# Layer 1 of a compressed-interaction tower regrouped by roll of h: four product tiles in full precision, twelve split in two, h's rolls passed through PSUM one after the other

## What is computed

```python
for i, (W, b) in enumerate(zip(Ws, bs)):
    z = jnp.einsum('bhd,bmd,ohm->bod', h, x, W.reshape(O, H, F))
    z = jax.nn.relu(z + b[None, :, None])
    if i < n_layers - 1:
        half = O // 2
        h, direct = (z[:, :half, :], z[:, half:, :])
    else:
        direct = z
    directs.append(direct)
out = jnp.concatenate(directs, axis=1)
return jnp.sum(out, axis=-1)
...
h = jnp.maximum(h @ W_top1 + b_top1, 0.0)
h = jnp.maximum(h @ W_top2 + b_top2, 0.0)
y = h @ W_top3
```

## Time and profile before

| quantity | value |
|---|---|
| runs of the kernel before | 1121.48, 1125.46 and 1120.56 us, median 1121.48 |
| the profiled execution | 1127.21 us |
| its span, from the first to the last instruction | 1125.4 us |
| granted TensorE clock, mean | 0.995 of full speed |
| busy, share of the span | PE 97%, DVE 92%, POOL 66%, ACT 53% |
| DMA | 162.97 MB, mean 145 GB/s |

### The profile page before, as it was taken

One profiled execution on the slowest core, in us unless ns is written; L12 is line 12 of the kernel. 1 busy time (PEld: TensorE's weight loads), 2 busy tenths in 40 slices (PEclk: granted clock), 3 DMA queues, 4 the chain that ended last, 5 costly groups with the idle time before them and its releaser, 6 DMA issues.

```text
span 1125.4 us, 11475 instructions
## 1 busy us (share of the span) xinstructions
PE 1086.0 (97%) x3562; PEld 660.5 (59%) x3562; DVE 1034.8 (92%) x580; ACT 597.8 (53%) x517; POOL 744.1 (66%) x333
## 2 busy tenths in 40 slices
PE   3789999999999999999999999999999999999997
PEld 1355655666565666656666666656665666656665
DVE  1589999999999999999999999999999999999993
ACT  0156555545654555565455556555545655555545
POOL 6466767777787777768777777877777787743110
PEclk9899999999999999999999999999999999999999
DMA  6665454665544466554446555544566554455200
GB/s 203 206 166 147 141 144 132 177 174 153 149 147 135 129 177 176 166 143 138 141 128 171 176 155 161 141 134 127 169 176 168 148 142 145 131 153 145 78 0 1
DMA packets 73576, 162.97 MB, mean 145 GB/s; under 512 B 14785, under 2 KB 39874, under 8 KB 73554
## 3 DMA queue, kind: packets, MB, share of 16 engines
q1 hardware_dynamic: 52738, 147.57, 46.2%
q10 hardware_dynamic: 12624, 10.92, 3.0%
q0 software_dynamic: 8192, 4.21, 2.3%
HBM read 95.52 MB, written 8.39 MB: 92 GB/s over the span
## 4 chain that ended last, share of the span: by engine, by line
PE 86%; DVE 6%; issue 2%; ACT 1%; DMA 1%; another core or an unknown queue 1%; ACTq 1%; POOL 1%; SPq 0%; DVEq 0%; POOLq 0%
PE z_ps L723 84%; DVE raw L591 2%; PE u_ps L723 2%; DVE prod L527 2%; DVE prod_lo L597 2%; DMA twice<-raw 1%; POOL gathered L364 1%; ACTq L1016 0%; ACT prod_hi L1097 0%; ACT h_roll L1083 0%; PE mlp_ps L723 0%; ACT h L969 0%; DMA gathered<-in_table,rows_sb 0%; DMA base_sb<-in_row_base 0%
## 5 line engine op out<-in xcount | busy, mean ns | idle before, releaser
L723 PE MATMUL z_ps<-prod,w_sb 128*128 128x512 f32 x1280 | 575.6, 596 | 10.8 <-ACT direct L959 4.0
L364 POOL DMA_INDIRECT gathered<-in_table,rows_sb x256 | 454.1, 1774 | 73.9 <-issue 68.3
L723 PEld LDWEIGHTS z_ps<-prod,w_sb 128*128 128x128 f32 x1280 | 243.6, 191 | 273.4 <-issue 262.3
L986 ACT CAST prod_hi<-raw 128x2048 fp32r<-128x2048 f32 x160 | 305.2, 1908 | 180.0 <-DVE raw L591 179.3
L591 DVE TENSOR_TENSOR raw<-h_roll,x_roll 128x2048 f32<-128x2048 f32 x160 | 363.4, 2288 | 1.2
L527 DVE TENSOR_TENSOR prod<-mlp_ps,x_roll 128x2048 f32<-128x2048 f32 x124 | 279.6, 2285 | 8.5 <-issue 5.7
L723 PE MATMUL z_ps<-prod_hi,w_hi 128*128 128x512 f32 x648 | 249.0, 464 | 3.5 <-DVE prod_lo L597 3.1
L375 POOL TENSOR_TENSOR prod_lo<-raw,prod_hi 128x2048 fp32r<-128x2048 f32 x32 | 146.8, 4587 | 135.4 <-DVE prod_lo L597 109.1
L597 DVE TENSOR_TENSOR prod_lo<-raw,prod_hi 128x2048 fp32r<-128x2048 f32 x98 | 223.9, 2286 | 1.0
L384 POOL TENSOR_TENSOR prod_lo<-raw,prod_hi 128x2048 fp32r<-128x2048 f32 x30 | 139.0, 4632 | 122.3 <-DVE prod_lo L597 122.3
L723 PE MATMUL z_ps<-prod_lo,w_hi 128*128 128x512 f32 x648 | 204.8, 396 | 0.0
...
## 6 DMA issues: line engine op xcount, KB each, us to landing
x_roll<-x_dram SPq DMA_DIRECT2D x128, 512.0 KB
...
twice<-raw ACTq DMA_DIRECT2D x128, 64.0 KB
...
```

The costliest lines, as they stand in the source:

```text
L364: nc.gpsimd.indirect_dma_start(gathered[:, u, g * DIM:(g + 1) * DIM], None, table, bass.IndirectOffsetOnAxis(ap=rows_sb[:, col:col + 1], a ...
L723: return nc.tensor.matmul(*args, **kw)
L986: nc.scalar.copy(prod_hi[:, SPLIT_SLOT[r], :, :], raw[:, RAW_SLOT[r], :, :]).then_inc(hi_ready, 1)
```

## The change

Layer 1's 16 tiles are grouped by roll of h. The four tiles of roll 0 are whole (two whole pairs, `products1`, which read h from SBUF), and the twelve tiles of rolls 1, 2 and 3 are split: six pairs A10, A12, A20, A22, A30, A32, where the first digit is the roll and the second the first of two x. ACT copies roll 1, 2 and 3 to `mlp_ps` in turn (`copy_roll`), each when the pairs of the roll before it are made, and x's base of chunk c+2 behind them. `raw` and `prod_hi` have four slots, `prod_lo` three, and `h_roll` has one copy rather than two. POOL now makes the rest of three pairs (A10, A20, A32) and DVE of three (A12, A22, A30). The half tile of layer 0 is made for chunk c+2 in step c. SP issues the rolls of h ahead of the loads of `x_roll`, and frees them by A30 and A32. The loads of the dense network's first weights move to the end. The core of the diff:

```diff
-WHOLE1 = 3
-B0, B1, A1, B2, B3 = range(5)
-SPLIT1 = 5
+WHOLE1 = 2
+A10, A12, A20, A22, A30, A32 = range(6)
+SPLIT1 = 6
 RING = 2
...
+RAW_SLOT = (0, 1, 2, 3, 0, 1)
+RAW_RING = 4
+HI_SLOT = (0, 1, 2, 3, 0, 1)
+HI_RING = 4
+LO_SLOT = (0, 1, 2, 0, 1, 2)
...
-    return SPLIT1 * c + (-1, 0, -2, 1, 2)[r]
+    return SPLIT1 * c + (-1, 0, -3, -2, 1, 2)[r]
+
+
+def used_before_lo(c, r):
+
+    return SPLIT1 * c + (-2, -1, 0, 1, 2, 3)[r]
...
+                wait(pool, split_used, used)
+                pool.wait_ge(window, opened)
+                nc.gpsimd.tensor_tensor(prod_lo[:, LO_SLOT[r], :, :], raw[:, RAW_SLOT[r], :, :],
+                                        prod_hi[:, HI_SLOT[r], :, :], ALU.subtract).then_inc(ready, 1)
...
-                if not_first(c) and pool_makes_lo3(c - 1 if isinstance(c, int) else c):
-                    lo3(c - 1)
+                if not_first(c) and pool_makes_last_lo(c - 1 if isinstance(c, int) else c):
+                    lo(c - 1, A32, lo_ready, lo_count(c - 1, A30), lo32_ready)
...
-                    if u == 1:
-                        make_rows(group + 1)
-                    gather(c + ahead, (u + ahead) % UNROLL, group if u == 0 else group + 1, 0)
-                lo1(c)
+                    gather(*after, range(0, 5))
+                if is_first(c):
+                    lo(c, A10, prod_ready, first1(c) + WHOLE1, lo10_ready)
+                else:
+                    lo(c, A10, direct_summed, c, lo10_ready)
                 if more:
-                    gather(c + ahead, (u + ahead) % UNROLL, group if u == 0 else group + 1, 1)
-
-            make_rows(0)
+                    gather(*after, range(5, 6))
+                lo(c, A20, lo_ready, lo_count(c, A12), lo20_ready)
+                if more:
+                    gather(*after, range(6, GATHERS))
...
-                if is_first(c):
-                    load_part16(c, s)
-                if not isinstance(c, int) or c != 1:
-                    load_base(c)
+                load_base(c)
+                if not is_first(c):
+                    load_part16(c)
+                if reuses:
+                    roll_h(c - 1)
...
-                        sp.wait_ge(*free[b])
+                        sp.wait_ge(raw_ready, free[b // PAIR])
...
+                dve.wait_ge(roll_copied[a], c + 1)
+                if r == A30:
+                    dve.wait_ge(lo10_ready, c + 1)
...
+                elif r == A20:
+                    dve.wait_ge(lo20_ready, c)
                 else:
-                    hs, xs = h_roll[:, s, PAIR:2 * PAIR, :], twice(x_roll[:, s, r - (r > A1), :])
-                nc.vector.tensor_tensor(raw[:, RAW_SLOT[r], :, :], hs, xs, ALU.mult).then_inc(raw_ready, 1)
+                    dve.wait_ge(lo_ready, lo_count(c - 1, {A10: A30, A12: A32, A22: A22}[r]))
+                nc.vector.tensor_tensor(raw[:, RAW_SLOT[r], :, :], twice(mlp_ps[:, :]), x_roll[:, s, k:k + PAIR, :],
+                                        ALU.mult).then_inc(raw_ready, 1)
...
+                wait(dve, split_used, used_before_lo(c, r))
...
+            def products1(c, u):
+
+                dve.wait_ge(h1_ready, 2 * (c + 1))
+                for k in range(PAIRS0):
+                    whole(first1(c) + k, slot1(c, u) + k, twice(h_roll[:, 0, :]),
+                          x_roll[:, u % 2, k * PAIR:(k + 1) * PAIR, :])
...
-                s = u % 2
                 if not is_last(c):
-                    products0(c + 1, (u + 1) % UNROLL, group if u < UNROLL - 1 else group + 1)
...
+                    products0(*later(c, u, group, 1))
+                    split_rest16(c + 1)
+                if not_first(c, 2):
+                    layer2(*later(c, u, group, -2))
...
-                split_product(c, u, B0)
-                if not is_first(c):
-                    rolled_once()
-                split_product(c, u, B1)
-                if not is_last(c):
...
-                dve.wait_ge(h0_copied, c + 1)
-                for k in range(PAIRS0):
-                    whole(first1(c) + 1 + k, slot1(c, u) + 1 + k, twice(mlp_ps[:, :]),
-                          x_roll[:, s, k * PAIR:(k + 1) * PAIR, :])
+                    products1(c, u)
+                split_product(c, u, A10)
+                split_product(c, u, A12)
                 if not_first(c):
-                    layer2(c - 1, *before)
-                    sum_direct(c - 1, *before)
-                split_product(c, u, A1)
-                split_product(c, u, B2)
-                split_rest(c, A1)
-                split_product(c, u, B3)
-                split_rest(c, B2)
-                if not pool_makes_lo3(c):
-                    split_rest(c, B3)
-                if u == 1 and not_first(c, UNROLL):
+                    products1(c, u)
+                    sum_direct(*later(c, u, group, -1))
+                if not isinstance(c, int) or c + 2 < CHUNKS:
+                    product16(*later(c, u, group, 2))
+                split_product(c, u, A20)
+                split_product(c, u, A22)
+                split_rest(c, A12)
+                split_product(c, u, A30)
+                split_product(c, u, A32)
+                split_rest(c, A22)
+                split_rest(c, A30)
+                if not pool_makes_last_lo(c):
+                    split_rest(c, A32)
+                if is_last(c):
+                    layer2(*later(c, u, group, -1))
+                if u == 2 and not_first(c, UNROLL):
                     sum_z2(group - 1)
...
-                if not_first(c) and pool_makes_lo3(c - 1 if isinstance(c, int) else c):
-                    split(z1_ps, c - 1, B3, stop=True)
+                if not_first(c) and pool_makes_last_lo(c - 1 if isinstance(c, int) else c):
+                    split(z1_ps, c - 1, A32, stop=True)
                 if not is_last(c):
                     layer0(*after, 1)
+                    layer0_pairs16(c + 1)
...
                 layer1(c, u, 0)
-                if not is_last(c):
-                    layer0_pairs16(c + 1)
-                    if not_first(c):
-                        layer2_u(c - 1, (u - 1) % UNROLL)
-                split(z1_of(c), c, B0)
-                if is_last(c):
+                layer1(c, u, 1)
+                if not_first(c):
                     layer2_u(c - 1, (u - 1) % UNROLL)
-                layer1(c, u, 1)
-                split(z1_of(c), c, B1)
-                layer1(c, u, 2)
-                split(z1_of(c), c, A1)
-                if u == 0 and not_first(c):
-                    layer2_sum(c, group - 1)
-                split(z1_of(c), c, B2)
-                if not pool_makes_lo3(c):
-                    split(z1_of(c), c, B3, stop=True)
+                if u == 1 and not_first(c, UNROLL):
+                    layer2_sum(c - 1, group - 1)
+                for r in (A10, A12, A20, A22, A30):
+                    split(z1_of(c), c, r)
+                if not pool_makes_last_lo(c):
+                    split(z1_of(c), c, A32, stop=True)
...
+                if not_first(c):
+                    act.wait_ge(prod_ready, first1(c - 1) + WHOLE1)
+                    for a in range(1, ROLLS):
+                        act.wait_ge(h1_rolled[a - 1], c * 32)
...
-
-                act.wait_ge(h1_ready, 2 * (c + 1))
-                if not_first(c):
-                    act.wait_ge(prod_ready, first1(c - 1) + WHOLE1 if is_last(c) else first0(c + 1) + PAIRS0)
-                nc.scalar.copy(mlp_ps[:, :], h_roll[:, u % 2, 0, :]).then_inc(h0_copied, 1)
+            def copy_roll(c, a):
+
+                act.wait_ge(h1_rolled[a - 1], (c + 1) * 32)
+                if a > 1:
+                    act.wait_ge(raw_ready, c * SPLIT1 + PAIR * (a - 1))
+                elif is_last(c):
+                    act.wait_ge(raw_ready, c * SPLIT1)
+                elif not_first(c):
+                    act.wait_ge(prod_ready, first0(c + 1) + PAIRS0)
+                nc.scalar.copy(mlp_ps[:, :], h_roll[:, a, :]).then_inc(roll_copied[a - 1], 1)
...
-                if not_first(c):
-                    copy_h0(c, u)
-                if not is_last(c):
-                    double_pairs16(c + 1)
-                round_products(c, B0)
-                if not is_last(c):
-                    round_pairs16(c + 1)
+                more = not isinstance(c, int) or c + 2 < CHUNKS
+                copy_roll(c, 1)
+                round_products(c, A10)
                 if not_first(c):
                     relu1(c - 1, (u - 1) % UNROLL)
-                round_products(c, B1)
+                copy_roll(c, 2)
+                round_products(c, A12)
                 if not is_last(c):
-                    relu0(c + 1, (u + 1) % UNROLL)
-                round_products(c, A1)
+                    relu0_h(c + 1)
+                if more:
+                    double_pairs16(c + 2)
+                round_products(c, A20)
+                copy_roll(c, 3)
+                round_products(c, A22)
                 if not is_last(c):
```

(17 more changed lines are left out.)

259 lines of the change are left out of this document (121 added, 138 removed).

## The result

The changed kernel takes 1174.27 us (median of 4 runs, 1173.89 to 1175.47), the kernel before 1122.83 in the same session (1120.56 to 1125.46): a ratio of 1.0459, 95% interval 1.0432 to 1.0486. Slower was right, the size was not: 1143 us was predicted and 1154 was the upper end.

A forecast was written before the change was run, and what follows sets the result against it. A loop of waits through DVE, POOL's subtraction for A20 and PE was to set 33.55 us a chunk. 29 steps take 973.0 us against 951.4, so 1121.5 + 21.6 = 1143 us, range 1122 to 1154.

The forecast's parts named there:

- PE sets the pace before; a split pair costs 2.80 us: PE, through the two `prod` slots, bounds the kernel before at 32.73 us a chunk; a split pair takes PE 2.80 us.
- The loop: Round of waits from DVE's second whole pair through POOL's subtraction for A20 and PE, back to DVE: 33.51 us; chance 0.70.
- half tile term: DVE's half tile, behind `sum_direct` and ahead of A20's product, counted as 0.33 us of the loop.
- POOL starts 0.15 behind the end of the rest: POOL's subtraction for A20 was to start 0.15 us after DVE's rest of A12 ends.
- the likeliest case: The A20 loop sets the chunk at 33.4 to 33.8 us, the kernel at 1136 to 1152 us; chance 0.70.
- The ends: The first step and the last two steps were to change nothing, within 3 us.
- difference carries over: The profiled execution before lay 5.7 us above the median; the same gap was assumed after, lowering 1148.8 to 1143 us.
- What the profile would show: PE idle before the third split pair, DVE before the second whole pair from SBUF; same instruction every 33.5 us.
- The second loop: Rival: the same round through DVE's rest of A22 binds at 32.7 us, no change, 1119 to 1125 us; chance 0.13.
- PE's pace: Rival: PE's own work still sets the chunk at 32.10 us, giving 1101 us; chance 0.06.
- Late loads of x: Rival: loads of x, all freed only by A30 and A32, hold up DVE, up to 1181 us; chance 0.08.
- The half tile behind POOL: Rival: DVE's half tile stands until POOL's subtraction for A10 ends, +4.5 us in the loop, 1270 us; chance 0.03.

The follow-up runs named there:

- experiment 5: On the changed kernel, DVE makes the half tile ahead of the two products of `products1` instead of behind the direct sum: 1173.44 us.
- experiment 7: PE runs A20's high-half records before its wait for POOL: changed kernel, 1154.85 us; kernel with gathers, half tile, direct sum and relu moved, 1123.33; A22 likewise there, 1110.78.

## Why the prediction was right in sign and wrong in size

- **PE sets the pace before; a split pair costs 2.80 us.** Right. After, whole and split pair take 706.73 - 700.50 = 6.23 us as in the earlier trace rows, and with the loops open the chunk is 32.11 us.
- **The loop.** Right in the members that it names: A22's records lie in it and A12's outside, by what leaving them out did. Its half tile term counts only together with POOL's subtraction for A10 beside it; the text had seen that rest and subtraction meet within 0.1 us, and experiment 5 shows that they are tied.
- **"POOL starts 0.15 behind the end of the rest."** This is the step that failed. It read POOL's gap from a place in the earlier trace rows where POOL had nothing else to do (it had waited 2.38 us). `gather(*after, range(5, 6))` stands in the changed code between the two subtractions, and was given no row and no price. The gap measured 0.86 us instead of 0.15, which is 0.71 us (11.21 against 10.50), 28 times, 20 us; taking the gather out gave 20 us back. The rows to price it stood in the trace of before. There an indirect DMA beside the product from `h_roll` of 546.59 ends 0.82 us behind it (549.70 against 548.88):

```profile
547.02 2.68 POOL L364 DMA_INDIRECT gathered<-in_table,rows_sb  x1 [0.31 <-issue]
```

- **The rest of the miss.** The upper end of the likeliest case, by its own 33.8 us, is 29 x 33.8 - 951.4 + 1121.5 + 3 = 1153 us and not 1152, which changes nothing. From 1143 to 1174.3 are 31.3 us. The 29 steps took 993.75 us between direct sums (96.31 to 1090.06) where 973.0 were predicted: 20.8, of which 19.9 are the gather and 1.5 the one chunk at the lower clock, less 0.6 for the rest. Measured by direct sums before's steps took 949.0 (100.63 to 1049.64), not 951.4: 2.4. The ends gave 2.5 together, inside the 3 allowed (the first steps -4.3, the last two +6.8). And the profiled execution of before lay 5.7 us above its median, which the text carried over; after's, 1174.36 beside a median of 1174.27, does not. So the "difference carries over" was a second step that failed, worth 5.7 us, and no run shows where those 5.7 us lie. Without the gather the prediction would have been 11 us too low and just inside its range (1153.92 against 1154).
- **What the profile would show.** PE idle 1.2 to 1.6 us: it was 1.75 to 1.80 (1.33 to 1.36 in each fourth chunk), and 1.09 to 1.13 (0.70) once the gather was gone. DVE idle 1.7 us: only 0.81 to 1.02, because beside POOL two rests behind the loop took 5.50 us for 4.40 and the half tile's rest 1.4 to 1.8 us where it took 0.69 before; in this kernel that cost nothing. PE 95%, POOL 78%: 92% and 75%.
- **Rivals.** The second loop was there and hidden behind the first, as experiment 7 shows, but it was no case of no change: with the gather in place it measured 33.64 us, not 32.7, because its rest of A22 was summed as if POOL's subtraction for A20 didn't hold it up. PE's pace (1101 us) needed both loops open. Late loads of x: from 400 to 900 us DVE had no wait for a load. The half tile behind POOL happened once, in step 0, 4.69 us at 59.59.
